# Second cross-attention of a perceiver: the output projection of a group of four batches begun one batch later

## The reference, cut to what matters

```python
xn = layer_norm(x, g_media, b_media)              # the context
ln = layer_norm(latents, g_latent, b_latent)      # the latents
q = (ln @ Wq).reshape(B, Q, 16, 64).transpose(0, 2, 1, 3) * scale
k, v = jnp.split(jnp.concatenate([xn, ln], axis=1) @ Wkv, 2, axis=-1)
sim = jnp.einsum('bhqd,bhfd->bhqf', q, k)         # 16 heads, 257 + 32 keys
sim = jnp.where(full_mask[:, None, None, :], max_neg, sim)
alphas = jax.nn.softmax(sim, axis=-1)
out = jnp.einsum('bhqf,bhfv->bhqv', alphas, v)
return out.transpose(0, 2, 1, 3).reshape(B, Q, HIDDEN) @ Wout + bout
```

## Time and profile before

| | us |
|---|---|
| median of three runs | 1198.02 |
| lowest and highest of them | 1193.25 and 1201.19 |
| the profiled execution, its own time | 1191.41 |
| its span, first to last instruction | 1188.8 |
| TensorE matmul, VectorE, ScalarE, GpSimd busy | 1028.6, 779.0, 711.5, 402.8 |

### The profile page before, as it was taken

The page is one execution under the profiler, slowest core; times in us unless marked ns, Lnnn a source line. Parts: engine busy times, 40 slices in busy tenths (PEclk is TensorE's granted clock), DMA queues, the critical chain, the costliest instruction groups (busy, mean ns, idle before and its releaser), DMA issues. The chain is left out here.

```text
span 1188.8 us, 38609 instructions
## 1 busy us (share of the span) xinstructions
PE 1028.6 (87%) x14222; PEld 806.9 (68%) x14222; DVE 779.0 (66%) x2840; ACT 711.5 (60%) x1725; POOL 402.8 (34%) x756
## 2 busy tenths in 40 slices
PE   5899999986767758887799999999999999887965
PEld 2688888853766547876578888888888887422443
DVE  3578888865687378884475666666656666365376
ACT  2588888853676437774465555555555554464467
POOL 0122222206452036664143434343434344112042
PEclk8799999998899679998899999999999999998978
DMA  1443334300000826664354545454545453000001
GB/s 52 117 122 80 80 80 80 80 11 1 1 1 2 310 78 197 216 195 128 86 127 114 132 118 131 121 128 118 130 113 135 114 130 105 28 0 0 1 1 35
DMA packets 71676, 109.83 MB, mean 92 GB/s; under 512 B 12512, under 2 KB 51360, under 8 KB 71424
## 3 DMA queue, kind: packets, MB, share of 16 engines
q1 hardware_dynamic: 69056, 103.06, 32.1%
q0 software_dynamic: 2496, 5.12, 1.6%
HBM read 92.79 MB, written 15.34 MB: 91 GB/s over the span
## 5 line engine op out<-in xcount | busy, mean ns | idle before, releaser
L1533 POOL TENSOR_TENSOR d_p<-d_p,d_rtotal 128x289 f32<-128x289 f32 x256 | 170.2, 665 | 254.8 <-DVE d_rtotal L1677 254.8
L1637 ACT ACTIVATE d_p<-d_p,d_nmax 128x289 f32<-128x289 f32 x256 | 137.7, 538 | 131.6 <-DVE d_nmax L1671 131.5
L1671 DVE CUSTOM_DVE_ANT_0 d_p<-bank,d_low 128x289 f32<-128x289 f32 x256 | 112.1, 438 | 150.6 <-PE bank L1564 150.6
L1578 PE MATMUL bank<-d_pT,d_xr 32*128 32x128 f32 x5120 | 160.9, 275 | 2.1 <-DVE d_a L1691 2.1
L1564 PE MATMUL bank<-x_keyT,d_q 128*128 128x289 f32 x512 | 158.2, 426 | 2.9 <-DVE d_nmax L1671 1.6
L1578 PEld LDWEIGHTS bank<-d_pT,d_xr 32*128 32x128 f32 x5120 | 148.8, 187 | 11.0 <-issue 3.9
L438 ACT ACTIVATE a_p<-a_p,a_nmax 128x257 f32<-128x257 f32 x256 | 116.2, 506 | 33.5 <-DVE a_nmax L475 31.7
L1685 DVE STREAM_TRANSPOSE d_pT<-d_p 128x320 f32<-128x320 f32 x256 | 128.1, 500 | 1.1 <-POOL d_p L1533 1.1
L475 DVE CUSTOM_DVE_ANT_0 a_p<-bank,a_low 128x257 f32<-128x257 f32 x256 | 93.8, 422 | 25.7 <-PE bank L388 23.7
L1564 PEld LDWEIGHTS bank<-x_keyT,d_q 128*128 128x128 f32 x512 | 82.0, 189 | 37.0 <-DVE d_nmax L1671 21.7
L445 ACT ACTIVATE a_pT<-bank 128x512 f32<-128x512 f32 x128 | 69.7, 594 | 20.6 <-PE bank L397 20.1
(11 more groups left out here) (334 smaller groups left out, 2105.4 us busy)
## 6 DMA issues: line engine op xcount, KB each, us to landing
d_xr<-key_rows SPq DMA_DIRECT2D x256, 160.0 KB, 3.1
d_low<-mask_low SPq DMA_DIRECT2D x64, 144.5 KB, 3.4
a_ctT<-in_ctxT SPq DMA_DIRECT2D x64, 128.5 KB, 2.1
a_low<-mask_low SPq DMA_DIRECT2D x64, 128.5 KB, 3.0
c_ct<-in_ctx SPq DMA_DIRECT2D x32, 256.0 KB
key_rows<-c_ct SPq DMA_DIRECT2D x32, 256.0 KB, 2.2
c_w<-in_L_ffn_w SPq DMA_DIRECT2D x8, 578.0 KB, 10.4
c_w<-expert_out SPq DMA_DIRECT2D x8, 256.0 KB, 4.5
```

Source lines behind the costliest of these rows:

```text
L1533: nc.gpsimd.tensor_tensor(p, p, rtotal[:, b % 2, g:g + 1].broadcast_to([128, KEYS]), ALU.mult).then_inc(normed, 1)
L1578: ins = nc.tensor.matmul((OL if latents else O)[j], xr[rows, b % 2, k, :], pT[rows, b % 2, :, 32 * k:32 * k + 32], start=(k == 0 or latent ...
L1637: nc.scalar.activation(p, p, ACT.Exp, bias=nmax[:, b % 2, g:g + 1], scale=-1.0, accum_out=total[:, b % 2, g:g + 1]).then_inc(exp_made, 1)
L1671: nc.vector.tensor_tensor_reduce(P[:, b % 2, g, 0:KEYS], S[u % 2], low[:, b % 4, :], -1.0, 3.4e38, ALU.add, ALU.min, accum_out=nmax[:, b % ...
```

## The change

TensorE starts each group's projection one batch later (batches 4n + 6 to 4n + 9). VectorE's addition moves from the second batch (behind the first unit's turn) to the third batch of a group, behind the second unit's maximum and ahead of its invert, turn and combine. In the first turn batch 5 has no projection. After the last turn TensorE does two quarters of group 14 (the third and the fourth) ahead of the last means, in place of one. No instruction is added or removed.

```diff
@@ TensorE @@
                 def project(i, b):
-                    ago, r = divmod(b - 5, 4)
+                    ago, r = divmod(b - 6, 4)
                     if r == 0:
                         pe.wait_ge(o_copied, (i * 2 + ago + 1) * 4)
                         if not (isinstance(i, int) and i * 2 + ago == 0):
@@
                         scores(i, b, 3, first)
-                        if not (first and b < 5):
+                        if not (first and b < 6):
                             project(i, b)
@@
                 unrolled(TURNS, body)
                 project(TURNS, 0)
+                project(TURNS, 1)
                 means(TURNS, -1)
                 for r in range(4):
-                    project(TURNS, 1 + r)
+                    project(TURNS, 2 + r)
@@ VectorE @@
                         maximum(i, u, first)
+                        if b % 4 == 2 and g == 1 and not first:
+                            project(i, (b - 10) // 4)
                         if not (first and u < 1):
                             invert(i, u - 1)
                         if not (first and u < 2):
                             turn(i, u - 2, first)
-                        if b % 4 == 1 and g == 0 and not first:
-                            project(i, (b - 9) // 4)
                         if g == 1 and i * EIGHT + b >= 2:
                             combine(i * EIGHT + b - 2)
```

## The result

The changed kernel takes 1189.62 us (median of 8 runs, 1184.47 to 1190.63) against 1198.05 for the kernel before (8 runs, 1193.25 to 1204.61). The ratio is 0.9906, 95% interval 0.9886 to 0.9926: 11.3 us less, 8.9 to 13.7. I had forecast 1185.0 and a saving of 13.0. The two medians by themselves are 8.4 us apart, less than the ratio on record gives for the same runs: whole times can't settle a saving of this size to a few us.

What follows compares the result with a forecast made beforehand. TensorE was taken to bound the stage, working in its own order. Savings of 12.5 + 1.0 less 0.4 at the tail, taken as 13.0 us, off the median 1198.02 gave 1185.0 us, range 1178 to 1194.

Steps and rivals of the forecast that it cites:

- What bounds the stage: Whole stage: TensorE counts, busy 19.63 of 20 us; VectorE and the DMA queue do not hold it back in general.
- Second batch, 14 x 0.89: Second batch of each group: no wait on combine, addition gone; 6.38 in place of 7.27 us, 12.5 us saved.
- Batch 5, 1.0: First turn: batch 5 loses its projection, its means wait for combine; 6.05 in place of 7.05, 1.0 us less.
- Third batch, 0, with slacks of 0.18 and 0.11: Third batches: no loss; addition's result seen at 2.67, deadline 2.85; means possible at 3.83, TensorE free at 3.94.
- Rival 1: Third batches: late addition or combine makes a new wait, up to 0.36 in each of 14; 1190.0 us; chance 0.12.
- DMA queue: Loads of d_xr: no DMA issued or passed; used 10.3 us after issue, landing after 3.1; margin shrinks 0.9.
- Tail, 0.4: End of stage: one more quarter before the last means loses 0.4 us, the other 0.6 fitting in the idle gap.
- The sum: Whole kernel: 12.5 + 1.0 - 0.4 = 13.1, taken as 13.0 us saved; 1185.0 us, 1.09% less.
- Rival 3, the clock behind the stage: Later stages: a further low-clock stretch costs up to 5.2 us, 1190.2, or goes the other way; dear side 0.08.
- the 3 us that I had named as a sign of being wrong: Behind the stage: the prediction is wrong if the time there changes by over 3 us.
- Rival 2: Second batches stay at 7.27 because something other than combine, such as scores waiting for maxima, holds TensorE; 1198; chance 0.06.
- rival 4: The stage itself loses the full clock as TensorE has no gap left; 1210 at 50 us low; chance 0.02.

Runs made afterwards that it cites:

- the last experiment, e7_turn_later: Changed kernel with the turn between a batch's first and second maximum put behind the second; stage 412.91 us, ratio to the kernel before 0.9895.
- e2_add_only: Kernel before with only its addition moved, to the last unit of the batch making the last quarter, projection unmoved; stage 424.98 us against 427.96.
- e6_tail: Changed kernel with the second of the two quarters ahead of the last means put behind them; stage 415.25 us, 0.4 longer.

## Why the prediction was right

- *What bounds the stage.* Right: TensorE in its own order. Ordinary batches stayed at 6.37 to 6.38 in every variant, and the last experiment shows that the one wait left in their rows costs nothing.
- *Second batch, 14 x 0.89.* Right: 12.33 measured against 12.5, and its split into the addition ahead of the maximum (0.22) and combine (0.67) is shown by e2_add_only.
- *Batch 5, 1.0.* Right: 1.00.
- *Third batch, 0, with slacks of 0.18 and 0.11.* The sum is right. The terms were a little off, and in part cancelled: the addition started at 2.22 and not 2.30, took 0.35 and not 0.31, and its end reached a waiting projection after 0.11 to 0.12 and not 0.06, so the result was seen at about 2.69 rather than 2.67. The deadline of 2.85 is borne out by the table. combine came at 2.97 (2.98 expected) and the means at 3.94. Rival 1 did not come about. But 0.36 a batch was no upper bound for a late addition: behind combine it cost 0.99 a batch, the whole gain and not 5.0 us.
- *DMA queue.* Right: TensorE's waits from 600 to 1000 list none for a load.
- *Tail, 0.4.* It was 0.21. This term was twice too large. I had added the spacing of a projection that had waited (1.09) and the whole length of a row of weight loads (1.10), which ends while the next row runs; two quarters in a row take 1.98 to the means, 0.99 each. That the addition of group 14 is covered was right, with 2.84 us to spare; e6_tail lost this cover.
- *The sum.* Stage 13.10 against 13.0. In time, the ratios give 11.3 (8.9 to 13.7) and 13.7 (10.3 to 17.1): both intervals hold 13.0. The median after lay 4.6 above my 1185.0, inside the range; nothing in the stage accounts for that, and the time ahead of and behind it wanders by more. A median nearer to or farther from 1185.0 would have been luck either way. That a saving of 13.0 lies near the 1% line was stated; the first measurement fell under it (0.94%), to which I had given 0.43, the second over (1.14%), to which I had given 0.55.
- *Rival 3, the clock behind the stage.* It exists in single executions: the kernel before had 169.97 and 169.15 us behind the stage, the changed one 169.72, 169.80 and 175.41. The last passes the 3 us that I had named as a sign of being wrong. The changed program has both values, so the later projection is not enough to bring the longer one about; whether it makes it more frequent is open. A spell of low clock comes without the change too: of eleven executions of the kernel before in one set, the two at a mean clock of 0.940 and 0.941 over the whole program took 1198.44 and 1195.69 us, the nine at 0.944 and above 1185.99 to 1194.01. They were not profiled, so where their spell lay is not known. The Trainium skill (TensorE: Matmul & The Clock Gate, "Part 1: The HAM clock gate") has the gate's schedule independent of the kernel's start; profiles of one kernel with clocks of 0.88 and 0.91 there agree with that.
- *Rival 2 and rival 4.* Neither: second batches 6.38, granted clock 1.00 over the whole stage. What rival 2 had in its favour, the fourth score's wait for the second maximum, costs an ordinary batch nothing (e7_turn_later).

What makes the time ahead of the stage wander by 17 us was not tried. The traces say where it arises: over the twelve profiles VectorE's 93rd record starts from 46.3 to 51.8 us, its 2025th from 408.6 to 415.5, and its 2669th, with the stage still ahead, from 531.4 to 547.2. So some 6 us arise in the first 50 us and most of the rest after 410.

## What to carry to other kernels

Where one engine works through its list without a gap, each wait can be given a deadline in the list of a neighbouring iteration that is not disturbed; a wait met before the deadline costs nothing (2.75 here), and what lies behind it is paid in full in each such iteration (0.33 and 0.99 here). Measure the length of the stage from its own first and last instruction: here it repeats to 0.1 us where whole times of one kernel spread over 6 to 12 us. Before a small operation is moved in one engine's list, follow what is queued behind it there, since a waiting addition of 0.35 us can hold a combine on which everything hangs.

## What the runs showed that I had not expected

- Idle time in front of a weight load is no loss by itself: 0.20 us in every ordinary batch went away and the batch gained 0.01.
- From the end of the addition in VectorE to the start of a waiting projection it is 0.11 to 0.12 us, twice the 0.06 of the wait for combine at the same matmul in the earlier trace rows.
- The same program reached its second cross-attention between 585.9 and 603.2 us, and the same changed kernel took 5.7 us more behind the stage in one execution than in another, at a granted clock of 0.88 in place of 0.91.
